# Batches 1 and 2 of a selective scan cut into halves, with every order written anew

## The reference

```python
# layer 1, per batch
xi = in_proj_w @ ctx.T                    # 512 x L
u = silu(causal_conv4(xi, conv_w) + conv_b)
dt_lo, Bm, Cm = split(x_proj_w @ u)       # 16, 16, 16 rows
delta = softplus(dt_proj_w @ dt_lo + dt_proj_b)
A = -exp(A_log)                           # 512 x 16
state = state * exp(delta_t * A) + (delta_t * u_t) * B_t   # for each step t
y_t = sum_n state[:, n] * C_t[n]
y = (y + D * u) * silu(layernorm(x))
x = x + tanh(g_xattn) * y
# layer 2, per token of n = layernorm(x): top 2 of 8 experts and a shared one
combine = normalised softmax weights of the two best of gate_w @ n
out = sum_e combine_e * wu_e @ gelu(wd_e @ n + bd_e) + combine @ bu + ws_u @ gelu(ws_d @ n + bs_d) + bs_u
x = x + tanh(g_ffn) * out
```

## Time and profile before

| | |
|---|---|
| time, median of 3 runs | 643.73 us (643.26 to 643.81) |
| the profiled execution's own time | 644.75 us |
| its span, first to last instruction | 643.0 us |
| TensorE matmul busy | 502.3 us, 78% of the span |
| VectorE busy | 505.0 us, 79% |
| GpSimd busy | 494.2 us, 77% |
| ScalarE busy | 396.6 us, 62% |
| DMA queue, share of 16 engines | 36.4% |

### The profile page before, as it was taken

How to read it: one execution, slowest core, us unless ns; L and a number is a source line. 1 busy time by engine, 2 the same in 40 slices (tenths; PEclk the granted TensorE clock), 3 DMA queues, 4 the chain that set the end, 5 groups by cost and what they waited for, 6 DMA issues and landing times.

```text
span 643.0 us, 7504 instructions
## 1 busy us (share of the span) xinstructions
PE 502.3 (78%) x2304; PEld 253.7 (39%) x2304; DVE 505.0 (79%) x560; ACT 396.6 (62%) x755; POOL 494.2 (77%) x240
## 2 busy tenths in 40 slices
PE   5605544787899698974399899974998999889988
PEld 4202211234564364610033333331443443657866
DVE  4477799878989999995879899958689879982211
ACT  4549656897926877474666854455689765681250
POOL 4199999999988959999979999978578799950000
PEclk9657757757989798966589989975999799899979
DMA  2596723374246150337720323075111553002101
GB/s 83 166 371 210 255 66 99 115 249 166 97 150 184 63 196 2 106 113 304 244 95 7 130 79 110 27 240 201 50 49 41 208 181 123 25 2 67 33 1 49
DMA packets 39940, 79.70 MB, mean 124 GB/s; under 512 B 5977, under 2 KB 12761, under 8 KB 39900
## 3 DMA queue, kind: packets, MB, share of 16 engines
q1 hardware_dynamic: 39900, 79.23, 36.4%
HBM read 62.17 MB, written 17.04 MB: 123 GB/s over the span
## 4 chain that ended last, share of the span: by engine, by line
DVE 34%; PE 27%; ACT 14%; issue 14%; POOL 7%; DMA 3%; ACTq 0%; DVEq 0%; SPq 0%; POOLq 0%
DVE decay L1229 11%; DVE ring L1229 8%; PE wk L1537 8%; PE wk L1523 7%; ACT decay L1064 5%; POOL ring L988 5%; DVE ring L1243 4%; PE y_ps L1458 3%; PE wk L1474 3%; DMA dd<-dd_scratch 2%; PE wk L1487 2%; ACT L1033 2%; POOL ring L1010 1%; DVE xc L1305 1%; ACT h L1163 1%
## 5 line engine op out<-in xcount | busy, mean ns | idle before, releaser
L988 POOL TENSOR_TENSOR ring<-dd,b_in 128x2048 f32<-128x2048 f32 x64 | 289.3, 4531 | 15.8 <-issue 13.1
L1064 ACT ACTIVATE decay<-dd,a_neg 128x255 f32<-128x255 f32 (+1 forms) x384 | 188.4, 533 | 37.3 <-DVE ring L1229 37.0
L1229 DVE TENSOR_TENSOR_SCAN ring<-decay,ring 128x1024 f32<-128x1024 f32 x64 | 144.4, 2277 | 16.1 <-ACT decay L1064 10.1
L1010 POOL TENSOR_TENSOR ring<-ring,c_in 128x2048 f32<-128x2048 f32 x32 | 144.9, 4527 | 13.1 <-DVE ring L1229 7.7
L1229 DVE TENSOR_TENSOR_SCAN decay<-decay,ring 128x1024 f32<-128x1024 f32 x64 | 146.3, 2285 | 8.5 <-ACT decay L1064 5.7
L1523 PE MATMUL wk<-xc,w_down 128*128 128x256 f32 (+1 forms) x432 | 139.4, 478 | 11.7 <-DVE xc L1311 6.0
L1537 PE MATMUL wk<-h,w_up 128*128 128x256 f32 (+1 forms) x432 | 137.2, 474 | 0.4 <-DVE h L1404 0.4
L1458 PE MATMUL y_ps<-ring,fold 128*32 128x256 f32 (+1 forms) x768 | 77.4, 547 | 64.3 <-DVE ring L1243 63.3
L1523 PEld LDWEIGHTS wk<-xc,w_down 128*128 128x128 f32 x432 | 84.3, 201 | 62.0 <-issue 46.6
L1537 PEld LDWEIGHTS wk<-h,w_up 128*128 128x128 f32 x432 | 84.3, 200 | 44.5 <-issue 35.1
L1243 DVE TENSOR_TENSOR ring<-decay,c_in 128x1024 f32<-128x1024 f32 x64 | 78.2, 1222 | 1.7
(11 more groups left out here) (104 smaller groups left out, 427.1 us busy)
## 6 DMA issues: line engine op xcount, KB each, us to landing
dd<-dd_scratch SPq DMA_DIRECT2D x64, 256.0 KB, 3.0
dd<-dd_scratch SPq DMA_DIRECT2D x32, 512.0 KB, 4.2
b_in<-bc_scratch SPq DMA_DIRECT2D x8, 512.0 KB, 5.0
c_in<-bc_scratch SPq DMA_DIRECT2D x8, 512.0 KB, 5.2
dd_scratch<-dd_out SPq DMA_DIRECT2D x16, 256.0 KB, 2.0
z<-in_x SPq DMA_DIRECT2D x4, 1024.0 KB, 7.0
x<-in_xT SPq DMA_DIRECT2D x4, 1024.0 KB, 7.8
dd_scratch<-dd_out SPq DMA_DIRECT2D x8, 512.0 KB, 3.1
```

Of the source, the lines that this page charges most:

```text
L988: nc.gpsimd.tensor_tensor(two, dd[:, j % DD_RING:j % DD_RING + 2, None, n:2 * n].broadcast_to([P, 2, TILES[v], n]), b_in[:, None, g % BC_R ...
L1010: nc.gpsimd.tensor_tensor(two, two, c_in[:, None, g % BC_RING].broadcast_to([P, 2, WIDE]), ALU.mult).then_inc(weighed_pool, 2)
L1064: last = nc.scalar.activation(decay[:, i % 2, q * n + 1:(q + 1) * n], dd[:, j % DD_RING, 1:n], ACT.Exp, scale=a_neg[:, c, r, k:k + 1])
L1229: last = nc.vector.tensor_tensor_scan(to, decay[:, i % 2], ring[:, i % RING], 0.0, ALU.mult, ALU.add)
```

## The change

Batches 1 and 2 are cut into halves too, so that there are eight units of 256 steps, and every row of `PLAN` is written anew. Code outside `UNITS` and `PLAN` stays as it is, and so does the number of slots, 128. The rows of the diff that matter here (the other rows of `PLAN` change in the same manner):

```diff
-UNITS = [(0, 0, 256), (0, 256, 256), (1, 0, 512), (2, 0, 512), (3, 0, 256), (3, 256, 256)]
+UNITS = [(0, 0, 256), (0, 256, 256), (1, 0, 256), (1, 256, 256), (2, 0, 256), (2, 256, 256), (3, 0, 256), (3, 256, 256)]
...
     "y": [
-        [-2.78, 7, 8.06, 14.03],
-        [19.9, 23.2, 28.46, 32.48],
-        [38.52, 40.22, 43.73, 48.35, 52.48, 56.65, 58.32, 63.42],
-        [68.35, 72.12, 75.93, 79.68, 83.79, 90.79, 94.34, 95.2],
-        [99.7, 103.71, 107.26, 113.72],
-        [119.34, 120.42, 124.09, 128.82],
+        [3.67, 7.76, 11.05, 15.27],
+        [22.33, 23.32, 31, 31.47],
+        [38.66, 42.41, 44.28, 47.67],
+        [51.94, 57.93, 61.81, 64.47],
+        [71.04, 73.48, 75.98, 79.49],
+        [84.25, 87.68, 93.23, 95.84],
+        [101.78, 106.31, 111.54, 111.96],
+        [119.37, 123.19, 126.71, 129.15],
     ],
...
     "in_proj": [
-        [-8.04, -7.79, -7.54, -6.95],
-        [-6.58, -6.24, -5.89, -3.16],
-        [4.43, 7.8, 13.1, 17.1],
-        [22.21, 33.78, 39.4, 39.81],
-        [40.98, 49.89, 57.27, 63.65],
-        [95.14, 95.29, 95.51, 95.55],
+        [-6.98, -6.73, -6.48, -5.89],
+        [-5.52, -3.16, -2.91, -2.65],
+        [6.14, 14.86, 15.04, 15.16],
+        [19.45, 22.04, 31.38, 33.05],
+        [43.15, 45.97, 46.19, 47.58],
+        [53.06, 58.43, 63.3, 64.02],
+        [71.96, 75.74, 78.94, 80.08],
+        [87.37, 90.71, 97.45, 97.53],
     ],
...
     "x_proj": [
-        [-5.45],
-        [3.85],
-        [20.69],
-        [42.08],
-        [80.72],
-        [106.96],
+        [-4.51],
+        [3.14],
+        [16.61],
+        [35.44],
+        [49.92],
+        [71.45],
+        [83.04],
+        [99.25],
     ],
...
     "dt": [
-        [-3.81, -3.47, -3.34, -2.91],
-        [5.28, 5.51, 6.83, 6.92],
-        [23.06, 24.08, 24.43, 25.39],
-        [57.5, 57.71, 58.06, 61.03],
-        [95.02, 95.04, 95.06, 95.18],
-        [107.9, 107.95, 108.09, 111.23],
+        [-3.81, -3.68, -3.56, -2.2],
+        [6.04, 6.34, 6.83, 7.05],
+        [17.91, 18.17, 18.85, 19.32],
+        [38.1, 38.23, 38.53, 44.14],
+        [50.88, 53.31, 53.7, 54.05],
+        [72.35, 76.75, 77.72, 78.09],
+        [83.87, 84.11, 85.82, 85.95],
+        [101.55, 102.64, 102.77, 103.04],
     ],
...
     "load_dd": [
-        [-2.2, -2.12, -2.03, -1.74, -1.57, -1.48, 0, 0.18, 1.5, 1.74, 4, 4.82, 5.89, 7.01, 8, 8.5],
-        [8.9, 10.52, 11.56, 12.96, 13.74, 14.46, 15.55, 16.96, 17.74, 18.46, 18.98, 20.98, 21.42, 22.55, 23.33, 24.62],
-        [25.9, 27, 27.65, 28.96, 29.74, 30.43, 34.53, 36.71, 37.5, 38.4, 43.22, 43.99, 45.69, 46.43, 51.44, 52.64],
-        [61.29, 61.38, 61.47, 61.57, 62.29, 62.48, 66.78, 69, 69.22, 69.68, 76, 76.88, 77.69, 78.43, 83.38, 84.38],
-        [95.3, 95.31, 95.33, 95.35, 95.36, 95.38, 95.67, 95.68, 98, 98.38, 98.8, 100.08, 101.77, 102.52, 104, 104.9],
-        [110.01, 110.11, 110.21, 110.32, 110.42, 110.52, 112, 113, 114.13, 114.23, 116, 116.13, 117.98, 118.55,
-         119.37, 120.97],
+        [-2.2, -2.12, -1.94, -1.85, -0.94, -0.86, 0, 0.1, 1.79, 1.85, 3.93, 4.96, 5.93, 6.38, 9.48, 9.65],
+        [10.12, 10.62, 11.45, 12.96, 13.89, 14.93, 16.06, 16.24, 18.38, 18.46, 20, 20.82, 21.89, 22.55, 24, 24.18],
+        [26, 26.68, 27.67, 28.96, 33.59, 33.62, 33.65, 33.95, 34.71, 35.01, 35.92, 36.58, 37.75, 38.41, 39.94, 40.96],
+        [42.47, 42.66, 43.52, 44.58, 46.12, 46.84, 47.62, 47.7, 49.38, 50.42, 52.01, 52.96, 53.95, 54.15, 56.22, 56.77],
+        [57.76, 59, 59.96, 60.8, 62, 62.85, 65.26, 65.29, 65.77, 65.8, 67.98, 68.94, 69.87, 70.81, 71.89, 72.66],
+        [75.08, 75.18, 75.52, 76.71, 79.17, 79.29, 79.81, 81.16, 81.34, 82.35, 83.63, 84.17, 85.72, 86.23, 88, 88.98],
+        [90.04, 91.17, 91.59, 92.96, 93.47, 97.04, 97.07, 97.16, 97.76, 97.84, 101.56, 102.83, 102.92, 103.12,
+         103.95, 104.81],
+        [105.59, 106.87, 107.56, 108.96, 110, 110.84, 111.55, 111.99, 114.16, 115, 117.32, 117.47, 117.75, 119.71,
+         119.9, 120.76],
     ],
...
     "du": [
         [-3.8, -3.6, -3.4, -3.2],
-        [6.2, 6.4, 6.8, 8.333],
-        [24.286, 24.429, 24.714, 24.857],
-        [58.5, 58.667, 58.833, 60.667],
-        [92.375, 92.5, 92.625, 92.75],
-        [108.333, 108.5, 108.667, 110.5],
+        [8.333, 8.5, 8.667, 16.5],
+        [18.5, 32.167, 32.667, 32.833],
+        [38.5, 38.75, 44.5, 46.333],
+        [52.5, 54.4, 54.6, 54.8],
+        [74.2, 78.2, 78.8, 80.5],
+        [84.5, 90.4, 90.6, 92.333],
+        [102.6, 102.8, 104.5, 106.5],
     ],
...
     "conv": [
-        [0.1, 0.2, 0.3, 0.4],
-        [0.5, 0.7, 0.8, 0.9],
-        [7.333, 9.5, 15.333, 19.667],
-        [24.75, 35.25, 41.25, 41.5],
-        [43.25, 51.333, 58.667, 64.75],
-        [96.25, 96.333, 96.417, 96.583],
+        [0.125, 0.25, 0.375, 0.5],
+        [0.625, 0.875, 2.6, 2.8],
+        [7.667, 16.333, 16.5, 16.833],
+        [24.667, 24.833, 32.625, 34.467],
+        [45.5, 47.333, 48.143, 50.1],
+        [54.667, 59.75, 64.8, 66.167],
+        [75.333, 77.5, 81.333, 83.2],
+        [88.6, 92.333, 98.867, 98.933],
     ],
...
     "gate": [
-        [4.667, 8.667, 14.5, 18.5],
-        [21.333, 25.5, 30.5, 34.875],
-        [41.75, 50.1, 58.333, 64.5],
-        [74.5, 81.857, 92.667, 96.167],
-        [101.5, 105.5, 108.364, 115.333],
-        [120.8, 122.667, 125.667, 128.161],
+        [8.333, 11.667, 15.667, 16.667],
+        [24.167, 28.333, 32.375, 32.75],
+        [40.333, 44.333, 48.429, 50.2],
+        [55.333, 61.5, 64.6, 66.083],
+        [72.25, 76.333, 80.2, 81.667],
+        [87.5, 91.5, 94.4, 97.5],
+        [106.5, 112.25, 112.75, 114.5],
+        [120.833, 126.5, 128.061, 128.182],
     ],
...
     "weigh": [
-        [0.333, 6.6, 10.5, 14.333],
-        [18.333, 22.5, 24.571, 30.333],
-        [34.333, 38.5, 44.667, 48.5, 50.667, 54.5, 58.333, 60.333],
-        [64.5, 70.5, 76.667, 78.5, 84.667, 86.5, 90.5, 92.25],
-        [100.5, 104.5, 106.667, 108.833],
-        [112.333, 118.333, 120.333, 128.5],
+        [4.5, 8.167, 12.4, 12.6],
+        [20.333, 20.667, 28.2, 28.6],
+        [32.333, 38.25, 42.667, 44.75],
+        [50.333, 54.2, 56.667, 62.4],
+        [66.667, 70.5, 74.6, 78.4],
+        [82.667, 86.333, 90.8, 92.667],
+        [102.2, 102.4, 110.167, 110.667],
+        [112.667, 120.5, 128.167, 128.5],
     ],
...
     "stats_z": [
-        [2.2, 2.4, 2.6, 2.8],
-        [],
-        [35.5, 35.625, 35.75, 35.875],
-        [67.286, 67.429, 67.571, 67.714],
-        [96.667, 96.75, 96.833, 96.917],
+        [1.333, 1.667, 2.2, 2.4],
+        [],
+        [34.133, 34.267, 34.333, 34.4],
+        [],
+        [66.583, 66.667, 66.75, 66.833],
+        [],
+        [98.6, 98.667, 98.733, 98.8],
         [],
     ],
...
```

More of the change, by code:

```diff
@@ L179 @@
-        [95.46],
-        [116.21],
-        [129.85],
+        [17.43],
+        [31.81],
+        [50.54],
+        [65.24],
+        [82.81],
+        [97.35],
+        [114.22],
+        [130.17],
     ],
     "mean": [
-        [20.57],
-        [39.29],
-        [64.77],
-        [95.61],
-        [119.25],
-        [130.2],
+        [18.06],
+        [33.01],
+        [51.02],
+        [65.34],
+        [83.97],
+        [97.98],
+        [114.71],
+        [130.59],
     ],
     "var_p": [
-        [22.05],
@@ L193 @@
-        [40.14],
-        [66.24],
-        [95.88],
-        [119.83],
-        [131.54],
+        [19.19],
+        [33.94],
+        [55.71],
+        [65.78],
+        [87.6],
+        [102.9],
+        [117.55],
+        [131.92],
     ],
     "var": [
-        [22.98],
-        [40.64],
-        [66.47],
-        [95.96],
-        [120.2],
-        [132.87],
+        [23.18],
+        [35.36],
+        [57.74],
+        [65.87],
+        [88.32],
+        [106.21],
+        [119.29],
+        [132.28],
@@ L206 @@
     ],
     "lg_t": [
-        [24.8],
-        [42.85],
-        [67.07],
-        [97.71],
-        [122.48],
-        [134.19],
+        [25.07],
+        [42.27],
+        [59.43],
+        [67.2],
+        [90.11],
+        [107.33],
+        [119.79],
+        [133.6],
     ],
     "lg": [
-        [25.52],
-        [43.2],
-        [69.06],
-        [98.43],
-        [123.41],
-        [134.84],
+        [31.35],
+        [47.38],
+        [65.28],
+        [78.17],
+        [93.19],
+        [111.33],
@@ L263 @@
     "z": [
-        [-1.66],
+        [-1.77],
         [],
-        [34.01],
-        [63.76],
-        [95.41],
+        [31.86],
+        [],
+        [65.18],
+        [],
+        [97.01],
         [],
@@ L271 @@
     "x": [
-        [-1.39],
+        [5.12],
         [],
-        [39.78],
-        [66.71],
-        [96.29],
+        [37.9],
+        [],
+        [65.72],
+        [],
+        [101.38],
         [],
@@ L407 @@
+        [20.333, 20.5, 20.833, 24.333],
+        [40.4, 40.6, 40.8, 47.4],
+        [52.667, 56.167, 56.333, 56.5],
+        [75.333, 79.333, 79.667, 79.833],
+        [86.25, 86.5, 88.167, 88.333],
+        [104.25, 104.5, 104.75, 107.333],
```

(99 more changed lines are left out.)

304 lines of the change are left out of this document (174 added, 130 removed), and 72 rows, old and new, of the table PLAN.

## The result

The changed kernel takes **619.52 us**, median of 4 runs (619.16 to 621.21), against 643.77 (643.26 to 644.36) beside it: a ratio of 0.9628, 95% interval 0.9609 to 0.9648. It is 24 us faster, where I forecast 6.8 slower, and outside my range. The profiled execution took 619.49 us, its span is 617.8.

A forecast was written before the change was run, and what follows sets the result against it. No engine alone bounds the slots; VectorE (88%) and GpSimd (89%) hold each other up. 22.8 + 2.9 + 4.0 - 3.9 - 15.0 - 4.5 + 0.5 = +6.8 us, giving 650.5 us; range 634 to 661.

The forecast's parts named there:

- -15.0: Slots: VectorE's waits for gates due before TensorE has summed fall from 18.3 us to 3.3; ends 0 and -18.
- -4.5: Slots: batch 3 no longer stalls at its start and some routing logits wait less, -4.5 us; ends 0 and -14.
- ScalarE's +4.0: Slots: VectorE's 15.8 us of waits for ScalarE's decays grow by a quarter, 4.0 us; ends 0 and 16.
- the places: New positions of jobs in the engines' queues: gate waits -15.0 us, batch 3's start and logits -4.5 us.
- Work on VectorE: Slots: split operations, state copies and routing add 22.8 us, two convolutions moved from the lead 2.9; nothing hidden.
- the tail's 0.3: Behind the last scan: the third gate and a product with C stand there, forecast +0.5 us.
- GpSimd's work, not added: Slots: some 16.4 us more on GpSimd, taken to run beside VectorE's 22.8 and so left out of the sum.
- rival D: Slots: ScalarE's bursts raise VectorE's decay waits by 16 us instead of 4, or gates stay late; 661 us, chance 0.20.
- TensorE (17 us hidden): Slots: narrower products, sums and projections add 17 us on TensorE, hidden in its 116 us of idle time.
- The lead (-3.9): Ahead of the first scan: TensorE's 3.88 us wait before dt goes, first scan earlier by 3.9 us; ends 0 and -6.
- The ceiling: Slots: VectorE and GpSimd can't both be above 91% busy; VectorE's idle time below 45 us would refute it.
- Rival B: Slots: new orders in GpSimd's queue pay for the work, its idle time falling to 30 us; 628 to 642.4, chance 0.35.

## Why the prediction was wrong

**VectorE's idle time in the slots (-15.0, -4.5 and ScalarE's +4.0), the step that failed.** I had the slots 10.2 us longer: 25.7 us more work and 15.5 less idle time. They are 22.5 shorter: 15.1 more work and 37.6 less idle time. So 10.6 us of the miss are work, and 22.1 are idle time that I kept. Of these, 16.9 are the waits for decays, where I had the sign wrong: +4.0, and they fell from 15.8 to 2.9. Another 5.0 are logits and the rest, 9.5 instead of 4.5. Gates were right, 15.2 for 15.0. I kept the decays on the count of ScalarE's work and the rest on counted distances, although I had read that "Most of this idle time is thus one of order, not of work." A wait is put down here to what ended it; that is an account and not a price, since a wait that is taken away can come back under another name.

An estimate of what the places gave in time: with the prices of the kernel before, the added work costs 14.3 x 0.45 + 10.7 x 0.30 + 64.9 x 0.11 = 16.8 us; the time fell by 24.2, 2.9 of it in the lead, 0.2 came back in the tail; so the places gave about 38 where I had 19.5 (by the intervals of the prices, 32 to 45). The estimate takes work spread evenly to stand for work in lumps. The two single parts put back show why a sum over rows must fail: 20 gates lose 33 us and eight products lose 32, each more than the whole gain. The places hold each other; none has a share of its own.

**Work on VectorE (22.8 + 2.9, counted in full).** Its total rose by 14.3 us, not 22.8: neighbours in the queue overlap by some 0.09 us (the first scan, 2.29 us from 33.60, is followed at 35.80; the 128 one-operand instructions are 25.7 us long in all and raised the total by 10.9 and 13.3), so a row of means overstates a cut. And each us of light work costs 0.45, not 1. With ScalarE's term the work was in the sum at 29.7 and by the prices is worth 16.8: 13 of the 31 us between forecast and result, the places the other 19; the lead's 1.0 too many and the tail's 0.3 go against each other.

**GpSimd's work, not added.** 10.7 us more instead of 16.4, 5.3 of it in the slots; at 0.30 it is worth 3. Leaving it out of the sum was a small error in the kernel before. In the changed one it would be a large one.

**ScalarE (+4.0, and rival D).** Its work rose by 64.9 us, near the 60 forecast, but the waits for decays fell by 12.9. That the new places put its bursts where VectorE has other work is argued: no run moved ScalarE's jobs alone. No run shows D either. The table loads went from 59 to 79, 20 more where I had 16, at 1283 ns each, 25.7 us; they are part of the 64.9 us, and at the prices of added work, 0.11 and 0.23, little of that shows in the time.

**TensorE (17 us hidden).** Hidden, but its size can't be read from the totals: matmul busy fell by 3.4 us with 752 more matmuls, while the granted clock over the span rose from 0.85 to 0.90.

**The lead (-3.9).** -2.9: the wait went, 0.56 us of another stayed, and the first outer product moved from 31.97 to 29.06.

**The ceiling.** I had said that with VectorE's idle time below 45 us "my reading that the two engines can't both be above 91% was wrong"; it is 28.5, and both are at 94%. Rival B had the mechanism and its number, GpSimd's 30 us of idle time (31.0), and ended at 628 because it still added all of GpSimd's 16.4 us to the slots, where 5.3 came. I gave its best form less weight because VectorE would be at 94%, which no row excluded and which it is.

## What to carry to other kernels

Where two engines are each below 90% and wait in turn, new orders can win from the idle time of both. Here the fullest engine's work plus the idle time of its better stages told where that ends, 31.0 us for 30, and today's share did not; that is one case. Price added work by what it does to the time, not by its length: a small dummy instruction in each slot gives a first price in one run, if it is of a kind that stays short beside the other engines, and it prices more work only. And in a tuned static order, look at what stands ahead of the producer's next job: eight products put early in its queue cost more here than the whole change gained.
